# Opening of a Mamba and FP4-FFN kernel: low weight halves on GpSimd, z projections between x projections, dt pieces behind taps

## The chip, the cores and the metric

The kernel is one program on one core of a Trainium2 chip. The metric is the device time of one execution in microseconds, as the median of several executions. The core has five engines with queues of their own: TensorE (PE), VectorE (DVE), ScalarE (ACT), GpSimd (POOL) and SyncE (SP), which here only issues DMAs. They meet through semaphores.

## The reference, cut to what matters

For 8 sequences of 512 tokens with 512 features: a Mamba-2 block, residual and layer norm, then a feed-forward block with 4-bit weights, residual and layer norm.

```python
zxbcdt = u @ in_proj_w.T                      # 512 -> 64 (dt) + 128 (B) + 128 (C) + 1024 (x) + 1024 (z)
z, xBC, dt_raw = split(zxbcdt)
xBC = silu(causal_conv4(xBC) + conv_b)        # depthwise, four taps over the tokens
dt = softplus(dt_raw + dt_bias)
y = chunked_scan(x, dt, -exp(A_log), B, C)    # chunks of 64 tokens, decays exp(cumsum(dt * A))
yg = (y + x * D) * silu(z)
x1 = layernorm(u + rmsnorm(yg) * norm_weight @ out_proj_w.T)
out = layernorm(x1 + rmsnorm((silu(x1 @ gate.T) * (x1 @ up.T)) @ down.T))
```

## The kernel before, in words

Phase 1 runs the Mamba block over the 8 sequences, phase 2 the feed-forward block. While sequence b is scanned (`body`, 32 slots, four for each of 8 chunks), the input projection of sequence b+1 is made between the scan's steps. The projection of sequence 0 has nothing to hide behind: it is the opening of the program, and the change is in it alone.

The input projection has 19 output tiles of up to 128 features by 512 tokens: dt, B, C, x0 to x7, z0 to z7. Each is 12 matmuls: 4 blocks of input features, times three products of half-precision parts (`w_hi*u_hi`, `w_hi*u_lo`, `w_lo*u_hi`). The tiles take the two PSUM banks `ps_in0` and `ps_in1` in turn, by their place in a list of uses. A bank is free again when its tile has been read:

- a B, C or x tile is read by ScalarE (`take_conv`: the fourth tap, scaled, with the bias, into `pre`) and then by VectorE (`taps`: the three other taps, each an add into `pre`, the three of them in a chain). The third tap of VectorE frees the bank.
- a z tile is read by ScalarE alone (`take_z`: silu into `zg`), which frees the bank.

The weights come in as f32 and are split in the opening. `W_BLOCKS` has five blocks of columns: block 0 (dt, B, C), 1 (x0 to x3), 2 (x4 to x7), 3 (z0 to z3), 4 (z4 to z7), each of four tiles k of 128 input features. ScalarE writes `w_hi` = f16(w * scale) (`weights_hi`), VectorE writes `w_lo` = f16(w * scale - w_hi) (`weights_lo`). PE waits for a block's two halves ahead of the first tile that needs it. The f32 weights lie in buffers that are used for other things later: `xs` and the last part of `pre` (blocks 0 to 2), `zg` (blocks 3 and 4). So ScalarE must not write x5 into `pre` before all of `w_lo` of block 2 is made, nor z0 into `zg` before all of block 4's.

The time steps dt go through 25 small operations on VectorE (128x256), in pieces: `dt_first`, `dt_second` with parts 0 to 4, `dt_third`. Parts 1 to 4 are called pieces 1 to 4 below. ScalarE adds an exponential, a logarithm (`ln_dt`, after piece 3) and the factors of the scan (`exp_cs`, after the first operation of piece 4). After `dt_third` SyncE stores the parts to DRAM and loads rows back for the scan.

The opening ends in `tail`: after x7, one silu over B and C and two over x (`silu_all`) must wait for the last tap; `a0`, `a1`, `a2` are transposes and a product of chunk 0 that ScalarE evicts, `e0`, `e1`, `e2` the first exponent matrices, whose exponentials are ScalarE's. Each engine works its queue in the order of the code. GpSimd has almost nothing to do in the opening: two maxima over the partitions, a third (`reduce_u(1)`) after VectorE's `measure_u(1)`, behind the last taps.

## Time and profile before

| | us |
|---|---|
| median of 3 runs (1782.76 to 1784.73) | 1783.25 |
| the profiled execution, its own time | 1782.91 |
| its span, first to last instruction | 1781.1 |
| PE busy in the span | 1626.2 (91%) |
| DVE, POOL, ACT busy | 1304.0, 1119.5, 930.2 |
| opening, up to the first exponential of the scan's own slots | 114.0 |

How to read it: the span is one execution taken by the hardware profiler. A row of the timeline has the start in us from the span's start, the length in us, the engine, the line, the operation, the tile written and the tiles read with their shapes, the number of instructions of which the row is made, and in brackets how long the engine stood idle before and what released it. The end of a matmul is modelled; consecutive matmuls overlap, so it is their starts that count. A row of the stage view has a stretch and its length, then busy time and number of instructions of PE, PE's weight loads, DVE, ACT and POOL, then the granted clock of TensorE (1.00 is 2.4 GHz, 0.50 is 1.2 GHz), the DMA share and GB/s. Lines are those of the kernel before.

### The profile page before, as it was taken

Reading aid. Unit: us, or ns where it says so; the run is one execution under the profiler, and the core shown is the slowest. Engines: PE = TensorE matmul, PEld = TensorE weight load, DVE = VectorE, ACT = ScalarE, POOL = GpSimd, SP = SyncE. Lnnn points to the kernel's source line nnn. Section 1 sums busy time; section 2 is a strip of 40 time slices with the busy share of each in tenths; the row PEclk is TensorE's granted clock in tenths of the full one; section 3 lists DMA queues with packets and bytes.
Section 4 is the critical chain, followed back from the end, with each engine's and each line's share of the span. In section 5 each row is a group of like instructions: output and inputs, shape, how many; then the busy total and the mean of one; then the engine's idle time right before and its main releaser. Section 6 shows DMA issues by size and latency. Waiting matters only on the chain.

```text
span 1781.1 us, 36900 instructions
## 1 busy us (share of the span) xinstructions
PE 1626.2 (91%) x11168; PEld 818.8 (46%) x11168; DVE 1304.0 (73%) x2016; ACT 930.2 (52%) x1647; POOL 1119.5 (63%) x1087
## 2 busy tenths in 40 slices
PE   2699999989998998998998998888999999999998
PEld 1245545535544544544554554543344444444443
DVE  5939858858867876975985886656777777777774
ACT  2454454354445445435436436325766666666662
POOL 0038738837936845863873882885777776667773
PEclk9889999999999998998999999888999999999999
DMA  6121151141133124014114115721111101101011
GB/s 228 46 57 29 27 120 45 23 107 52 28 76 91 24 56 113 17 45 120 29 27 114 52 23 117 195 27 48 36 47 38 60 29 55 54 30 60 24 36 60
DMA packets 214697, 109.81 MB, mean 62 GB/s; under 512 B 133796, under 2 KB 185696, under 8 KB 214496
## 3 DMA queue, kind: packets, MB, share of 16 engines
q1 hardware_dynamic: 214496, 107.37, 22.5%
q8 instruction: 97, 1.59, 0.4%
q14 instruction: 104, 0.85, 0.2%
HBM read 80.57 MB, written 26.76 MB: 60 GB/s over the span
## 4 chain that ended last, share of the span: by engine, by line
PE 54%; issue 14%; DVE 12%; POOL 11%; ACT 4%; DMA 1%; SPq 1%; DVEq 0%; POOLq 0%; ACTq 0%
PE ps_in L770 12%; PE ps_in L924 8%; PE ps_yo L939 6%; PE ps_yd L939 6%; PE ps_in L792 6%; PE ps_s L924 4%; PE ps_t L924 4%; POOL xend L1665 4%; DVE pre L1270 3%; POOL y L1685 2%; PE ps_yo L850 2%; POOL y L1679 2%; DVE mix L1358 2%; PE ps_yd L840 1%; POOL sq L1702 1%
## 5 line engine op out<-in xcount | busy, mean ns | idle before, releaser
L770 PE MATMUL ps_in<-u_hi,w_hi 128*128 128x512 f16 (+1 forms) x608 | 234.3, 385 | 60.6 <-DVE u_lo L1257 32.4
L1665 POOL TENSOR_TENSOR xend<-xpad,decay 128x256 f32<-128x256 f32 x256 | 223.8, 894 | 102.9 <-PE ps_yo L863 47.1
L1075 ACT ACTIVATE decay<-ps_d 128x512 f32<-128x512 f32 x256 | 149.5, 592 | 243.6 <-PE ps_d L828 151.6
L792 PE MATMUL ps_in<-w_out,zg 128*128 128x512 f32 x512 | 230.8, 604 | 3.0 <-DVE pre L1270 2.5
L770 PE MATMUL ps_in<-u_lo,w_hi 128*128 128x512 f16 (+1 forms) x608 | 233.5, 384 | 0.0
L770 PE MATMUL ps_in<-u_hi,w_lo 128*128 128x512 f16 (+1 forms) x608 | 233.2, 383 | 0.0
L1358 DVE TENSOR_TENSOR mix<-decay,gb 128x1024 f32<-128x1024 f32 x128 | 179.3, 1401 | 49.3 <-ACT decay L1075 35.1
L1763 POOL TENSOR_TENSOR gate_sum<-gate_sum,gate_part 128x512 f32<-128x512 f32 x88 | 142.2, 1616 | 104.4 <-DVE gate_part L1586 104.0
L1270 DVE SCALAR_TENSOR_TENSOR pre<-ps_in,cws,pre 128x511 f32<-128x511 f32 (+2 forms) x240 | 179.2, 747 | 14.4 <-ACT pre L1014 8.1
L792 PEld LDWEIGHTS ps_in<-w_out,zg 128*128 128x128 f32 x512 | 95.8, 192 | 134.7 <-issue 124.2
L924 PE MATMUL ps_in<-xt_hi,gu_w 128*128 128x512 f16 x352 | 134.4, 382 | 5.5 <-DVE gate_sum L1586 2.3
L924 PE MATMUL ps_in<-xt_lo,gu_w 128*128 128x512 f16 x352 | 134.2, 381 | 0.0
L770 PEld LDWEIGHTS ps_in<-u_hi,w_hi 128*128 128x128 f16 (+1 forms) x608 | 60.8, 100 | 146.0 <-issue 46.4
L1014 ACT ACTIVATE pre<-ps_in,cb,cws 128x512 f32<-128x512 f32 x80 | 62.3, 778 | 121.7 <-PE ps_in L770 121.3
L1763 POOL TENSOR_TENSOR up_sum<-up_sum,up_part 128x512 f32<-128x512 f32 x88 | 113.0, 1284 | 14.6 <-DVE up_part L1586 14.1
L1679 POOL TENSOR_TENSOR y<-xs,dskip 128x512 f32<-128x512 f32 x64 | 80.4, 1256 | 56.5 <-issue 56.5
L850 PE MATMUL ps_yo<-bc,state 128*128 128x64 f32 x896 | 114.0, 281 | 0.9 <-DVE state L1374 0.9
L828 PE MATMUL ps_d<-rhs_d,lhs_d 94*128 94x512 bf16 x256 | 103.8, 406 | 6.9 <-DMA lhs_d<-ld_dram 6.0
L850 PEld LDWEIGHTS ps_yo<-bc,state 128*128 128x128 f32 x896 | 106.2, 194 | 6.2 <-DVE state L1374 1.2
L1671 POOL TENSOR_TENSOR state_d<-state,dec 128x1024 f32<-128x1024 f32 x48 | 104.6, 2178 | 0.0
L1771 POOL TENSOR_TENSOR h_lo<-hf,h_hi 128x512 f16<-128x512 f32 x88 | 103.1, 1172 | 0.3 <-ACT h_hi L1199 0.3
L1586 DVE SCALAR_TENSOR_TENSOR gate_part<-ps_in,gs,gate_part 128x512 f32<-128x512 f32 x88 | 66.0, 751 | 45.0 <-ACT gate_part L1185 35.5
(181 smaller groups left out, 3732.3 us busy)
## 6 DMA issues: line engine op xcount, KB each, us to landing
ebc<-e_dram SPq DMA_DIRECT2D x256, 64.0 KB, 2.7
u<-u_t SPq DMA_DIRECT2D x9, 1024.0 KB, 4.9
res<-u_tok SPq DMA_DIRECT2D x32, 256.0 KB, 3.7
x_dram<-res SPq DMA_DIRECT2D x32, 256.0 KB, 2.1
xa<-x_dram SPq DMA_DIRECT2D x8, 1024.0 KB, 5.8
xr<-x_dram SPq DMA_DIRECT2D x32, 256.0 KB, 2.6
out<-xr SPq DMA_DIRECT2D x32, 256.0 KB, 2.1
fw_words<-gu_words SPq DMA_DIRECT2D x32, 176.0 KB, 4.4
```

Of the source, the lines that this page charges most:

```text
L770: last = mm(ps_in[bk][0:m, :], w[:, k, col:col + m], u[:, k, :], start=(k == 0 and j == 0), stop=(k == KT - 1 and j == 2))
L792: last = mm(ps_in[bk][:, :], zg[:, k, tt * P:(tt + 1) * P], w_out[:, k, :], start=(k == 0), stop=(k == CT - 1))
L850: last = mm(ps_yo[:, k * CH:(k + 1) * CH], state[:, k * P:(k + 1) * P], bc[:, 1, c * CH:(c + 1) * CH], start=True, stop=True)
L924: last = mm(ps_gu[u % len(ps_gu)][:, :], gu_w[:, g, col:col + P], x[p.par][:, g, :], start=(j == 0), stop=(j == 1))
L939: last = mm(ps_n[tt % 2][:, :], h[par][:, k, tt * P:(tt + 1) * P], w[:, k, :], start=(step == 0), stop=(step == TILE_MMS - 1))
L1075: ac(decay[:, n % NG, :, :].rearrange("p a b -> p (a b)"), ps_d[n % 2][:, :], ACT.Exp).then_inc(e_done, 1)
L1270: ins = v.scalar_tensor_tensor(pre[:, m, d:L], ps_in[bk][:, 0:L - d], cws[:, m, k:k + 1], pre[:, m, d:L], ALU.mult, ALU.add)
L1358: v.tensor_tensor(mix[:, g:g + 2, :, :].rearrange("p g e t -> p (g e) t"), decay[:, g:g + 2, :, :].rearrange("p g e t -> p (g e) t"), gb[: ...
L1665: g_.tensor_tensor(xend[:, pairs, :], xpad[:, c % 2, pairs, :], decay[:, g, :, CH - 1:CH].broadcast_to([P, CT, 2 * HD]), ALU.mult).then_in ...
L1671: g_.tensor_tensor(state_d[:, :].rearrange("p (q d) -> p q d", d=HD), state[:, :].rearrange("p (q d) -> p q d", d=HD), dec[:, :, c:c + 1]. ...
L1679: g_.tensor_tensor(y[:, c % 2, :, :], xs[:, :, c * CH:(c + 1) * CH], dskip[:, :].unsqueeze(2).broadcast_to([P, CT, CH]), ALU.mult).then_in ...
L1763: g_.tensor_tensor(to[:, buf, :], to[:, buf, :], part[:, buf, :], ALU.add).then_inc(part_done, 1)
```

## The change

Three things are changed in the opening, and nothing else.

- `w_lo` of blocks 2, 3 and 4 (12 instructions of 128x512) is made by GpSimd. GpSimd gets a plain subtraction of two operands, so its f32 operand must already be scaled: ScalarE multiplies each f32 row block by `scale` in place (12 more activations, `weights_scaled`), right after the two or four `w_hi` that it makes from it. GpSimd waits for each tile's `w_hi` and for its scaled rows. ScalarE makes these blocks in smaller groups, between `take_conv` of C to x3.
- The order of the tiles is dt, B, C, x0 to x4, z0, x5, z1, x6, z2, x7, z3, z4, and then z5, z6, z7; `a0` comes after z4, and e0, a1, e1, a2, e2 after z7. Before, the order was x0 to x7, z0, a0, z1, z2, e0, a1, e1, z3, a2, e2, z4 to z7. The banks still alternate.
- VectorE makes the taps of x0 and x1 ahead of piece 1, the taps of x2 ahead of piece 2, those of x3 ahead of pieces 3 and 4, and `dt_third` after the taps of x5. ScalarE's `ln_dt` and `exp_cs` stand together after x4, ahead of z0.

```diff
@@ -73,10 +73,11 @@
 
 
 HEAD = ["a0", "z1", "z2", "e0", "a1", "e1", "z3", "a2", "e2", "z4", "z5", "z6", "z7"]
-TAIL = {"pro": ["x7", "z0"] + HEAD, "body": ["x6", "x7", "z0", "o3", "q3"] + HEAD, "last": ["o3", "q3"]}
+PRO_ORDER = ["dt", "B", "C", "x0", "x1", "x2", "x3", "x4", "z0", "x5", "z1", "x6", "z2"]
+TAIL = {"pro": ["x7", "z3", "z4", "a0", "z5", "z6", "z7", "e0", "a1", "e1", "a2", "e2"], "body": ["x6", "x7", "z0", "o3", "q3"] + HEAD, "last": ["o3", "q3"]}
 AUX_ORDER = (0, 2, 1)
 NA = len(AUX_ORDER)
-PRO_USES = [(0, "dt"), (0, "B"), (0, "C")] + [(0, f"x{i}") for i in range(CT - 1)]
+PRO_USES = [(0, name) for name in PRO_ORDER]
 BODY_USES = [(4, "dt"), (5, "B"), (7, "C"), (9, "x0"), (11, "x1"), (12, "o0"), (13, "q0"), (17, "x2"), (19, "x3"),
              (20, "o1"), (21, "q1"), (25, "x4"), (27, "x5"), (28, "o2"), (29, "q2")]
 LAST_USES = [(12, "o0"), (13, "q0"), (20, "o1"), (21, "q1"), (28, "o2"), (29, "q2")]
@@ -365,6 +366,7 @@
         w_out_done = sem("w_out_done")
         w_hi_done = sem("w_hi_done")
         w_lo_done = sem("w_lo_done")
+        w_scaled = sem("w_scaled")
         u_in = sem("u_in")
         res_in = [sem(f"res_in{tt}") for tt in range(TT)]
         rq_in = [sem("rq_in0"), sem("rq_in1")]
@@ -1125,10 +1127,16 @@
                     elif name[0] == "z":
                         take_z(st, name)
 
-            def weights_hi(block):
+            def weights_hi(block, tiles=range(KT)):
                 col, n = W_BLOCKS[block]
-                for k in range(KT):
+                for k in tiles:
                     ac(w_hi[:, k, col:col + n], w_src(k, col, n), ACT.Identity, scale=w_in_scale).then_inc(w_hi_done, 1)
+
+            def weights_scaled(block, tiles):
+                col, n = W_BLOCKS[block]
+                weights_hi(block, tiles)
+                for k in tiles:
+                    ac(w_src(k, col, n), w_src(k, col, n), ACT.Identity, scale=w_in_scale).then_inc(w_scaled, 1)
 
             act.wait_ge(small_in, N_SMALL)
 
@@ -1142,18 +1150,21 @@
             exp_dt(0)
             take_conv(pro, "B")
             take_conv(pro, "C")
-            weights_hi(2)
-            for i in range(CT - 1):
-                if i == 5:
+            weights_scaled(2, range(2))
+            for name in PRO_ORDER[3:]:
+                if name == "x5":
 
                     act.wait_ge(w_lo_done, KT * 3)
-                take_conv(pro, f"x{i}")
-                if i == 2:
+                if name[0] == "z":
+                    take_z(pro, name)
+                    continue
+                take_conv(pro, name)
+                i = int(name[1])
+                if i < 4:
+                    weights_scaled(*((2, range(2, KT)), (3, range(2)), (3, range(2, KT)), (4, range(KT)))[i])
+                if i == 4:
                     ln_dt(0)
-                if i == 4:
                     exp_cs(0)
-                if i in (3, 5):
-                    weights_hi(i // 2 + 2)
             act.wait_ge(const_in, N_CONST)
             act.wait_ge(pro_pool, 1)
             tail(pro)
@@ -1554,16 +1565,16 @@
             taps(pro, "C")
             dve.wait_ge(const_in, N_CONST)
             v.tensor_scalar(to_top[:, :], shift[:, :], 28, None, ALU.bitwise_xor)
-            dt_second(0, 1)
-            weights_lo(2)
-            for i in range(CT):
-                if i < 3:
-                    dt_second(0, 2 + i)
-                if i == 3:
-                    dt_third(0)
+            taps(pro, "x0")
+            for i in range(1, 4):
                 taps(pro, f"x{i}")
-                if i in (3, 5):
-                    weights_lo(i // 2 + 2)
+                dt_second(0, i)
+            dt_second(0, 4)
+            taps(pro, "x4")
+            taps(pro, "x5")
+            dt_third(0)
+            taps(pro, "x6")
+            taps(pro, "x7")
             measure_u(1)
             dve.wait_ge(w_out_in, 16)
             for k in range(CT):
@@ -1750,6 +1761,14 @@
             reduce_u(0)
             pool.wait_ge(pro_dve, MAXES_READY)
             g_.partition_all_reduce(maxes_all[:, :], maxes[:, :], P, RMAX).then_inc(pro_pool, 1)
+            pool.wait_ge(w_lo_done, 2 * KT)
+            for block in range(2, len(W_BLOCKS)):
+                col, n = W_BLOCKS[block]
+                for k in range(KT):
+                    pool.wait_ge(w_hi_done, KT * block + k + 1)
+                    pool.wait_ge(w_scaled, KT * (block - 2) + k + 1)
+                    g_.tensor_tensor(w_lo[:, k, col:col + n], w_src(k, col, n), w_hi[:, k, col:col + n], ALU.subtract)\
+                        .then_inc(w_lo_done, 1)
             reduce_u(1)
             body(Stage("body", 0))
             with pool.Fori(1, nb - 1) as i:
```

ScalarE before, from the taking of B and C on (`pre<-ps_in` is `take_conv`, `w_hi<-` is `weights_hi`):

```order
L1014 ACTIVATE pre<-ps_in,cb,cws 128x512 x2
L1131 ACTIVATE w_hi<-xs,scal 128x512 x3
L1131 ACTIVATE w_hi<-pre,scal 128x512
L1014 ACTIVATE pre<-ps_in,cb,cws 128x512 x3
L1006 ACT_TABLE_LOAD
L1006 ACTIVATE dtc<-dta 128x256
L1014 ACTIVATE pre<-ps_in,cb,cws 128x512
L1131 ACTIVATE w_hi<-zg,scal 128x512 x4
L1014 ACTIVATE pre<-ps_in,cb,cws 128x512
```

ScalarE now, the same place (`xs<-xs`, `pre<-pre` and `zg<-zg` are the scalings in place):

```order
L1016 ACTIVATE pre<-ps_in,cb,cws 128x512 x2
L1133 ACTIVATE w_hi<-xs,scal 128x512 x2
L1139 ACTIVATE xs<-xs,scal 128x512 x2
L1016 ACTIVATE pre<-ps_in,cb,cws 128x512
L1133 ACTIVATE w_hi<-xs,scal 128x512
L1133 ACTIVATE w_hi<-pre,scal 128x512
L1139 ACTIVATE xs<-xs,scal 128x512
L1139 ACTIVATE pre<-pre,scal 128x512
L1016 ACTIVATE pre<-ps_in,cb,cws 128x512
L1133 ACTIVATE w_hi<-zg,scal 128x512 x2
L1139 ACTIVATE zg<-zg,scal 128x512 x2
L1016 ACTIVATE pre<-ps_in,cb,cws 128x512
```

Each taking of an x tile now stands behind four activations, up to x3; eight more (block 4) stand between x3 and x4.

VectorE before, from the taps of C (a set of taps is three rows, 511, 510 and 509 elements) to the taps of x0:

```order
L1270 SCALAR_TENSOR_TENSOR pre<-ps_in,cws,pre 128x509
L1556 TENSOR_SCALAR to_top<-shift 128x1
L1290 TENSOR_TENSOR dtb<-dtb,dtd 128x256
L1291 TENSOR_TENSOR dtc<-dtb 128x256
L1292 TENSOR_SCALAR dtd<-dtc 128x256
L1293 TENSOR_TENSOR dtd<-dtd,dtc 128x256
L1543 SCALAR_TENSOR_TENSOR w_lo<-xs,scal,w_hi 128x512 x3
L1543 SCALAR_TENSOR_TENSOR w_lo<-pre,scal,w_hi 128x512
L1296 SCALAR_TENSOR_TENSOR dtd<-dtd,dtc 128x256 x5
L1270 SCALAR_TENSOR_TENSOR pre<-ps_in,cws,pre 128x511
L1270 SCALAR_TENSOR_TENSOR pre<-ps_in,cws,pre 128x510
L1270 SCALAR_TENSOR_TENSOR pre<-ps_in,cws,pre 128x509
```

VectorE now, from the last tap of x0 on:

```order
L1281 SCALAR_TENSOR_TENSOR pre<-ps_in,cws,pre 128x509
L1281 SCALAR_TENSOR_TENSOR pre<-ps_in,cws,pre 128x511
L1281 SCALAR_TENSOR_TENSOR pre<-ps_in,cws,pre 128x510
L1281 SCALAR_TENSOR_TENSOR pre<-ps_in,cws,pre 128x509
L1301 TENSOR_TENSOR dtb<-dtb,dtd 128x256
L1302 TENSOR_TENSOR dtc<-dtb 128x256
L1303 TENSOR_SCALAR dtd<-dtc 128x256
L1304 TENSOR_TENSOR dtd<-dtd,dtc 128x256
L1281 SCALAR_TENSOR_TENSOR pre<-ps_in,cws,pre 128x511
L1281 SCALAR_TENSOR_TENSOR pre<-ps_in,cws,pre 128x510
L1281 SCALAR_TENSOR_TENSOR pre<-ps_in,cws,pre 128x509
L1307 SCALAR_TENSOR_TENSOR dtd<-dtd,dtc 128x256 x5
```

The four `w_lo` and piece 2 stood ahead of the taps of x0; now those of x0, x1 and x2 come ahead of piece 2, and the `w_lo` are gone.

GpSimd before, at the program's start (`umax_all` and `maxes_all` are the maxima over the partitions; a row named ISA without a tile is an instruction that the program puts ahead of a first use of another kind):

```order
L1655 ISA umax_all<-umax 128x1
L1752 ISA maxes_all<-maxes 128x3
L1655 ISA umax_all<-umax 128x1
L1679 ISA
L1679 TENSOR_TENSOR y<-xs,dskip 128x512
L1665 TENSOR_TENSOR xend<-xpad,decay 128x256 x4
```

GpSimd now:

```order
L1666 ISA umax_all<-umax 128x1
L1763 ISA maxes_all<-maxes 128x3
L1770 ISA
L1770 TENSOR_TENSOR w_lo<-xs,w_hi 128x512 x3
L1770 TENSOR_TENSOR w_lo<-pre,w_hi 128x512
L1770 TENSOR_TENSOR w_lo<-zg,w_hi 128x512 x8
L1666 ISA
L1666 ISA umax_all<-umax 128x1
L1690 ISA
L1690 TENSOR_TENSOR y<-xs,dskip 128x512
```

The twelve subtractions stand ahead of the third maximum, with one more such ISA row ahead of them and one more ahead of that maximum.

## Rows read from the trace of the kernel before

**Rows 1.** Stage view: end of the waits inside the opening; first scan.
```profile
57.00:65.00 8.00, 7.54 (x24) 2.73 (x24) 7.58 (x15) 2.90 (x4) 0.00 (x0) 0.72 0.00 0
...
130.00:231.00 101.00, 97.77 (x842) 53.64 (x835) 85.38 (x119) 45.84 (x86) 76.77 (x81) 1.00 0.13 33
```

**Rows 2.** Timeline, TensorE: first matmul of x1, first of x2, last of x2.
```profile
47.94 0.39 PE L770 MATMUL ps_in<-u_hi,w_hi 128*128 128x512 f16 x1 [1.50 <-DVE pre L1270]
...
56.92 0.61 PE L770 MATMUL ps_in<-u_hi,w_hi 128*128 128x512 f16 x1 [6.21 <-DVE pre L1270]
...
61.57 0.38 PE L770 MATMUL ps_in<-u_hi,w_lo 128*128 128x512 f16 x1
```

**Rows 3.** Timeline, VectorE: pieces of dt, low halves and taps, x0 to x2.
```profile
47.86 0.42 DVE L1290 TENSOR_TENSOR dtb<-dtb,dtd 128x256 f32<-128x256 f32 x1
...
49.59 2.08 DVE L1543 SCALAR_TENSOR_TENSOR w_lo<-xs,scal,w_hi 128x512 f16<-128x512 f32 x3
...
52.25 2.26 DVE L1296 SCALAR_TENSOR_TENSOR dtd<-dtd,dtc 128x256 f32<-128x256 f32 x5
54.54 2.31 DVE L1270 SCALAR_TENSOR_TENSOR pre<-ps_in,cws,pre 128x511 f32<-128x511 f32 x3
56.78 0.41 DVE L1298 SCALAR_TENSOR_TENSOR dtd<-dtd,dtb 128x256 f32<-128x256 f32 x1
...
58.40 2.32 DVE L1270 SCALAR_TENSOR_TENSOR pre<-ps_in,cws,pre 128x511 f32<-128x511 f32 x3
60.63 0.68 DVE L1306 TENSOR_TENSOR_SCAN dte<-mask,dtb 128x256 f32<-128x256 bf16 x1
...
62.81 2.31 DVE L1270 SCALAR_TENSOR_TENSOR pre<-ps_in,cws,pre 128x511 f32<-128x511 f32 x3
```

**Rows 4.** Timeline, ScalarE: high halves, x1 taken, silus, first exponentials, z7, slot 0's exponential.
```profile
43.68 1.93 ACT L1131 ACTIVATE w_hi<-xs,scal 128x512 f16<-128x512 f32 x3
...
50.74 0.78 ACT L1014 ACTIVATE pre<-ps_in,cb,cws 128x512 f32<-128x512 f32 x1 [3.49 <-PE ps_in L770]
...
84.64 1.06 ACT L1025 ACTIVATE bc<-pre 128x1024 f32<-128x1024 f32 x1 [1.09 <-DVE pre L1270]
85.60 3.69 ACT L1027 ACTIVATE xs<-pre 128x2048 f32<-128x2048 f32 x2
...
98.64 0.60 ACT L1075 ACTIVATE decay<-ps_d 128x512 f32<-128x512 f32 x1
...
101.38 0.60 ACT L1075 ACTIVATE decay<-ps_d 128x512 f32<-128x512 f32 x1
...
112.01 0.69 ACT L1038 ACTIVATE zg<-ps_in,uundo 128x512 f32<-128x512 f32 x1 [1.90 <-PE ps_in L770]
...
114.01 0.60 ACT L1075 ACTIVATE decay<-ps_d 128x512 f32<-128x512 f32 x1
```

**Rows 5.** Timeline of the first scan: VectorE's rows, then GpSimd's.
```profile
132.66 2.31 DVE L1270 SCALAR_TENSOR_TENSOR pre<-ps_in,cws,pre 128x511 f32<-128x511 f32 x3
...
144.10 0.85 DVE L1290 TENSOR_TENSOR dtb<-dtb,dtd 128x256 f32<-128x256 f32 x1
144.98 1.15 DVE L1291 TENSOR_TENSOR dtc<-dtb 128x256 f32<-128x256 f32 x1
...
132.82 1.28 POOL L1685 TENSOR_TENSOR y<-y,yoff 128x512 f32<-128x512 f32 x1 [1.47 <-DVE yoff L1385]
...
143.06 1.61 POOL L1665 TENSOR_TENSOR xend<-xpad,decay 128x256 f32<-128x256 f32 x1
144.63 1.22 POOL L1679 TENSOR_TENSOR y<-xs,dskip 128x512 f32<-128x512 f32 x1
```

**Rows 6.** GpSimd: duration of `h_lo` in phase 2 (ns, min/median/max); timeline of the opening.
```profile
L1771 POOL TENSOR_TENSOR h_lo<-hf,h_hi x88: 1144/1157/1353, 1229.1 to 1749.3; 128x512 f16<-128x512 f32 x88
...
95.19 1.03 POOL L1679 TENSOR_TENSOR y<-xs,dskip 128x512 f32<-128x512 f32 x1 [7.57 <-issue]
...
115.27 2.02 POOL L1679 TENSOR_TENSOR y<-xs,dskip 128x512 f32<-128x512 f32 x1
```

## Prediction

> **What bounds the kernel now.** I read the stage view first. In the scan's stages TensorE is full: 97.77 of 101.00 us at a clock of 1.00 [rows 1]. Whatever the opening saves is therefore kept by the end if the scan only starts earlier, and nothing else in the program changes. In the opening TensorE is not the bound. The timeline of TensorE shows x1's projection at 47.94 and x2's only at 56.92, after 6.21 us of idleness that a tap of VectorE ended [rows 2]; the timeline of VectorE shows what it did meanwhile: piece 1 (47.86), four `w_lo` (49.59), piece 2 (52.25), and only at 54.54 the taps of x0, which free x2's bank [rows 3]. The opening is a chain of VectorE's work up to the last tap, then of the silus, then of the z tiles: silus from 84.64 to 89.29, z7 taken at 112.01, the exponential of slot 0 at 114.01 [rows 4]. That last row is my mark: all that follows it is the same work in both kernels. The question is when it starts now.
>
> **Prices.** Two projections stand 2.59 apart when nothing stops them (z7's taking: 1.90 idle and 0.69 of the one before) [rows 4]. From a projection's first matmul to its taking it is 2.80 (47.94 to 50.74), the taking is 0.78, a set of taps holds VectorE 2.24 (54.54 to 56.78), and the bank's next projection starts 2.38 after the taps began (54.54 to 56.92) [rows 2 to 4]. So x tiles that share one bank follow each other at 2.80 + 0.78 + 0.03 + 2.38 = 6.0 us, and a z tile (2.59) fits beside each. Pieces 1 to 4 hold VectorE 1.73, 2.29, 1.62 and 2.18 (the differences of neighbouring starts) [rows 3]. ScalarE starts its weight activations 0.61 apart (1.93 for three, overlapping by a tenth) [rows 4]. The scaling in place is not in the trace; between the 0.61 of `w_hi` and the 1.06 of the silu that writes f32 at twice the size [rows 4] I take 0.61, since shape and function are those of `w_hi`. GpSimd's `w_lo` has the form of `h_lo` (f32 and f16 in, f16 out, 128x512): 1144 to 1353 ns, median 1157 [rows 6]; the other end is the 2.02 of a product of that size that met VectorE [rows 6]. I take 1.16.
>
> **VectorE, x1 to x4.** The taps of C end at 47.86 as before; those of x0 follow at once and end at 50.1. x1 was projected at 47.94 and is taken at 50.74, so its taps start at 51.55. From there VectorE doesn't pause until x4's taps end: four sets of taps and four pieces, 4 x 2.24 + 1.73 + 2.29 + 1.62 + 2.18 = 16.8, to 68.35. The ScalarE work in between is not late: after x3 is taken (about 57) eight activations take 4.9, so x4 is taken at 62.7, and its taps come at 66 at the earliest. x4 needs block 2's `w_lo`, which GpSimd makes between 45.6 and 51.5; its projection starts at 58 or later. Block 3 is ready by 59, z0's projection comes at 62 or later.
>
> **What GpSimd costs VectorE.** In the scan, the multiplication of piece 1 at 144.10 takes 0.85 instead of 0.42; GpSimd's `xend` ends at 144.67 and VectorE 0.28 later. The next, at 144.98, takes 1.15: GpSimd's `y` ends at 145.85 and VectorE again 0.28 later [rows 3, 5]. So the pieces stand still while a GpSimd operation runs and do their streaming after it. Taps keep their 2.31 beside GpSimd's 132.82 row [rows 5]. The trace behaves as the Trainium skill states (SBUF — State Buffer, "Who interferes with whom"): a VectorE instruction with two SBUF inputs and a GpSimd one that reads SBUF exclude each other for a whole instruction. By that rule the change pays the loss worked out next; if the two engines did not exclude each other it would pay nothing, and the gain would be 3.35 larger. Walking the queues: block 3's first two `w_lo` run from 53.4 to 55.7, just when piece 1 starts (53.8); two of its operations wait, 1.5 us. Piece 2 then ends beside block 4's first `w_lo` (about 61): 0.9. Piece 3 begins beside the last: 0.95. Together 3.35, with bounds of 0 (no meeting) and 5.2 (each of about five waits a whole operation of 1.16, less what overlaps). x4's taps end at 71.7, x5's projection starts at 71.8.
>
> **TensorE's clock.** z0's projection is over by 68 or 69, so TensorE stands idle about 4 us ahead of x5. After 6.21 us of idleness it came back at half clock: x2's first matmul is 0.61 long, its last at 61.57 is back at 0.38, and the stage has 0.72 [rows 1, 2]. x2 took 4.65 from first to last start against 2.38 (2.59 less one start) at full clock, 2.3 more. For x5 I take 1.5: between 0 and 2.5, which all twelve at half clock would cost.
>
> **x5 to the mark.** x5 is as if started at 73.3; x6 at 79.3, x7 at 85.3 (two cycles of 6.0; `dt_third`, z1 and z2 lie beside them). Its last tap ends 2.80 + 0.81 + 2.24 later, at 91.15. That is 6.5 later than the 84.64 of before, but z0, z1, z2 are done and z3, z4 projected. The silus take 4.65 (84.64 to 89.29) [rows 4]: 95.8. z3 is taken (0.69), which frees the bank of z5: 96.5. Three projections, 7.8: z7's taking starts at 104.5, 0.2 after its last matmul. Then 0.69, a table load (112.01 + 0.69 to 114.01 leaves 1.3) [rows 4]: 106.5. The four exponentials, which before had their first three among the z tiles, now all stand behind z7: from 98.64 to the end of the third, 101.98, is 3.34 [rows 4], and transposes at half clock after the waits may add 0.4. The mark: 110.3 instead of 114.0, a gain of 3.7.
>
> **Costs at nothing, and their cover.** SyncE stores the dt parts about 14 us later (`dt_third` ends near 81.5), and needs about 15 us until the scan's rows are in SBUF, near 96.5; e0 asks for them near 104.5. The cover is 8 us. GpSimd's third maximum waits for `measure_u(1)`, over at about 93.5. A switch of kind costs 7.57 at 95.19 [rows 6]; two of them and the maximum end near 108.5, and `y` and the four `xend` near 112. New state is wanted some 7 us after the mark, so 5 us are left. z0's taking waits for all twelve `w_lo`, near 66, while ScalarE reaches it at 70. VectorE's `w_out` work (3.3) ends near 97.
>
> **The sum.** Without the meeting and the clock the gain would be 3.7 + 3.35 + 1.5 = 8.5; less 3.35, less 1.5: 3.7 us. Against its own time of 1782.91 that is 1779.2. The median of the runs shown is 0.34 higher, so 1779.5.
>
> **The rivals.**
> A, as forecast: gain 1.8 to 5.5. Chance 0.60.
> B, the meeting costs little, because VectorE's pieces fall between GpSimd's operations, or the clock stays up for x5: gain 5.5 to 8.5, time 1774.8 to 1777.8. For it: GpSimd is busy only 14 of the 20 us in question. Against: block 4's four run back to back into piece 3. Chance 0.20.
> C, the change moves nothing that can be told: each `w_lo` takes the 2.02 of the row at 115.27 [rows 6], so that each of four waits grows by 0.86, 3.4 in all; gain 0.3, time 1783. For it: that row shows how GpSimd itself is held. Against: VectorE's taps, most of its work there, do not hold it. Chance 0.15, with a gain between -3.6 and 1.8.
> D, slower: TensorE stays at half clock past x5. Each projection at 5.12 instead of 2.59 on the path (x5, x6, x7, z5, z6, z7) costs 2.5; one and a half more of them eat the gain, and with four more, 10.1, the time is 1789.6. It is slower by more than 0.2% from three more on. For it: every pair of tiles leaves TensorE idle 0.8 of 6.0 us, and it stands before x5 and before a0. Against: each return to work in rows 2 was back at full speed after under 5 us. Chance 0.05.
>
> **How the numbers follow.** 0.2% (3.6 us) is about what a measurement of this kernel can tell. Faster by more: half of A, the upper half of its range, and all of B: 0.5. Slower: D, 0.05. The rest, 0.45, is the lower half of A and C. The range leaves out the top of B, D, and most of C: 1776.5 to 1782.8.
>
> **What would show it.** TensorE's first x2 matmul near 50.5 instead of 56.92. VectorE unbroken from 51.5 to about 71.7, with single operations of pieces 1, 2 and 3 at 1.1 to 1.5 us instead of 0.42 beside `w_lo`. `w_lo` on GpSimd near 1.16, the last over near 66. x5 at half clock for its first part. The last tap near 91, silus after it; z7 taken near 104.5, slot 0's exponential near 110.3. The forecast is wrong if the scaling in place takes more than 1.0 (x4 would then be taken some 3 us later, at the edge of its taps), if SyncE's rows come after 104.5, or if the scan does not keep what the opening gives.

## The result

The changed kernel takes 1774.35 us (median of 5, 1773.86 to 1775.74), the kernel before 1784.73 (5 runs, 1782.76 to 1786.14). The ratio is 0.9944, interval 0.993 to 0.9959: 10 us faster, where 3.7 were forecast. The time lies below the range. The profiled execution is the one of 1774.35, its span 1772.5.

The stage view of the changed kernel, in the stretches of [rows 1]; columns are the length, then busy us (and count) of PE, PEld, DVE, ACT and POOL, TensorE's granted clock, the DMA share and GB/s:

```profile
57.00:65.00 8.00, 5.73 (x19) 2.07 (x20) 7.69 (x12) 6.50 (x10) 5.63 (x5) 0.79 0.01 2
130.00:231.00 101.00, 97.50 (x824) 52.32 (x823) 87.25 (x121) 44.65 (x83) 75.24 (x80) 1.00 0.13 33
```

GpSimd now works 5.63 of the 8 us in which it did nothing. The scan's stage looks as before. The timeline of TensorE (start, length, engine, line, operation, idle before and its releaser), first matmuls of x3, x4, z0, x5 and x6, with the last of x4 (62.08) and of x5 (75.13) and one of z5 (99.68) between them, answers to [rows 2]:

```profile
52.72 0.39 PE L772 MATMUL ps_in<-u_hi,w_hi 128*128 128x512 f16 x1 [0.63 <-DVE pre L1281]
58.31 0.38 PE L772 MATMUL ps_in<-u_hi,w_hi 128*128 128x512 f16 x1 [2.83 <-DVE pre L1281]
...
62.08 0.63 PE L772 MATMUL ps_in<-u_hi,w_lo 128*128 128x512 f16 x1
63.68 0.38 PE L772 MATMUL ps_in<-u_hi,w_hi 128*128 128x512 f16 x1 [0.96 <-DVE pre L1281]
70.46 0.61 PE L772 MATMUL ps_in<-u_hi,w_hi 128*128 128x512 f16 x1 [4.03 <-DVE pre L1281]
...
75.13 0.63 PE L772 MATMUL ps_in<-u_hi,w_lo 128*128 128x512 f16 x1
...
79.05 0.39 PE L772 MATMUL ps_in<-u_hi,w_hi 128*128 128x512 f16 x1 [0.36 <-DVE pre L1281]
...
99.68 0.63 PE L772 MATMUL ps_in<-u_hi,w_lo 128*128 128x512 f16 x1
```

x2 no longer waits, x3 waits 0.63. x4 waits 2.83, and its last seven matmuls ran at half clock (0.63 for a matmul instead of 0.38); that was off the path, because x4 was taken at 62.76 and VectorE came to its taps only at 68.10. x5 comes after 4.03 us of idleness at half clock, and all of its twelve stay there. The timeline of VectorE (answers to [rows 3]), then of GpSimd:

```profile
52.58 1.15 DVE L1301 TENSOR_TENSOR dtb<-dtb,dtd 128x256 f32<-128x256 f32 x1
53.76 1.27 DVE L1302 TENSOR_TENSOR dtc<-dtb 128x256 f32<-128x256 f32 x1
...
58.08 3.10 DVE L1307 SCALAR_TENSOR_TENSOR dtd<-dtd,dtc 128x256 f32<-128x256 f32 x5
61.21 2.32 DVE L1281 SCALAR_TENSOR_TENSOR pre<-ps_in,cws,pre 128x511 f32<-128x511 f32 x3
63.45 1.26 DVE L1309 SCALAR_TENSOR_TENSOR dtd<-dtd,dtb 128x256 f32<-128x256 f32 x1
...
68.10 2.31 DVE L1281 SCALAR_TENSOR_TENSOR pre<-ps_in,cws,pre 128x511 f32<-128x511 f32 x3
```

```profile
48.03 1.16 POOL L1770 TENSOR_TENSOR w_lo<-xs,w_hi 128x512 f16<-128x512 f32 x1 [1.16 <-ACT xs L1139]
...
52.29 2.46 POOL L1770 TENSOR_TENSOR w_lo<-zg,w_hi 128x512 f16<-128x512 f32 x2 [1.99 <-ACT zg L1139]
55.40 2.55 POOL L1770 TENSOR_TENSOR w_lo<-zg,w_hi 128x512 f16<-128x512 f32 x2 [0.66 <-ACT zg L1139]
59.74 4.68 POOL L1770 TENSOR_TENSOR w_lo<-zg,w_hi 128x512 f16<-128x512 f32 x4 [1.79 <-ACT zg L1139]
```

The pieces that meet GpSimd's `w_lo` are long, the taps beside the same rows keep 2.31. `w_lo` takes 1.16. ScalarE's timeline (answers to [rows 4]):

```profile
91.23 1.06 ACT L1027 ACTIVATE bc<-pre 128x1024 f32<-128x1024 f32 x1 [2.38 <-DVE pre L1281]
...
101.00 0.69 ACT L1040 ACTIVATE zg<-ps_in,uundo 128x512 f32<-128x512 f32 x1 [3.31 <-PE ps_in L772]
...
106.19 0.69 ACT L1040 ACTIVATE zg<-ps_in,uundo 128x512 f32<-128x512 f32 x1 [1.90 <-PE ps_in L772]
106.89 1.28 ACT L1077 ACT_TABLE_LOAD   x1
108.19 0.60 ACT L1077 ACTIVATE decay<-ps_d 128x512 f32<-128x512 f32 x1
...
110.89 1.08 ACT L1077 ACTIVATE decay<-ps_d 128x512 f32<-128x512 f32 x2
```

The mark (the fourth exponential, the second of the last row) starts at 111.39 instead of 114.01. That is 2.6 of the 8.6 us between the two spans. The rest came behind the mark. I cut the traces at rows that all kernels have, and each column is the length from one to the next: the mark, VectorE's measuring of `u` in the first scan and in the seventh (six scans between them), and the first gate matmul of phase 2. Plain copies of both kernels were run with the first experiments.

| trace | mark | to measuring of u | six scans | to gate | rest | span |
|---|---|---|---|---|---|---|
| before | 114.01 | 118.5 | 852.7 | 127.9 | 568.0 | 1781.1 |
| ctrl_before | 115.14 | 120.1 | 855.0 | 128.8 | 568.3 | 1787.4 |
| after | 111.39 | 117.5 | 846.9 | 128.1 | 568.6 | 1772.5 |
| ctrl_after | 111.39 | 119.8 | 848.9 | 130.5 | 568.9 | 1779.5 |

Six scans, in which the two programs do the same work, are 5.7 to 6.1 us shorter. In the mean of a trace all distances between ScalarE's exponentials agree to 0.1 us, but for two: the one across the loop's jump back (15.83 and 15.86 in the two traces of before, 15.19 and 15.23 in the two of after), and the one from the eighth to the ninth exponential of a scan, near the end of a stretch at half clock (5.89 and 5.86 against 5.54 and 5.71). At the jump ScalarE's table load waits. Before, then after, at the third jump, with the take of z7 ahead:

```profile
533.74 0.69 ACT L1038 ACTIVATE zg<-ps_in,uundo 128x512 f32<-128x512 f32 x1 [1.90 <-PE ps_in L770]
538.29 1.28 ACT L1075 ACT_TABLE_LOAD   x1 [3.86 <-issue]
```

```profile
528.68 0.69 ACT L1040 ACTIVATE zg<-ps_in,uundo 128x512 f32<-128x512 f32 x1 [1.90 <-PE ps_in L772]
532.39 1.28 ACT L1077 ACT_TABLE_LOAD   x1 [3.02 <-issue]
```

"issue" means that the profile shows no semaphore or engine that held it. The mean over the five jumps of a trace is 3.79 and 4.12 in the two of before, 3.09 and 3.37 in the two of after. That is 0.72 a jump, 3.6 us in all.

### The profile page after: what moved, and what is told of

Its sections match the earlier page's. It is cut to its first block, busy times and chain, and to the rows that moved or that the text cites. A ratio compares the mean times of both kernels' runs of the same rounds, so it can differ in the third digit from the quotient of the medians.

```text
span 1772.5 us, 36925 instructions
## 1 busy us (share of the span) xinstructions
PE 1625.4 (92%) x11168; PEld 818.0 (46%) x11168; DVE 1299.6 (73%) x2004; ACT 934.0 (53%) x1657; POOL 1134.6 (64%) x1099
## 3 DMA queue, kind: packets, MB, share of 16 engines
q8 instruction: 97, 1.59, 0.4%
## 4 chain that ended last, share of the span: by engine, by line
PE 53%; issue 14%; POOL 12%; DVE 12%; ACT 4%; DMA 1%; SPq 1%; POOLq 0%; DVEq 0%; ACTq 0%
PE ps_in L772 12%; PE ps_in L926 8%; PE ps_yo L941 6%; PE ps_yd L941 6%; PE ps_in L794 5%; POOL xend L1676 4%; PE ps_s L926 4%; PE ps_t L926 4%; DVE pre L1281 3%; POOL y L1696 2%; PE ps_yo L852 2%; POOL y L1690 2%; DVE mix L1369 2%; PE ps_yd L842 1%; POOL sq L1713 1%
```

## The experiments

**Parts of the change.** `pool_dt` has the change without its order of tiles; `pool_only` without the moved dt pieces too, so that the twelve `w_lo` on GpSimd and the scaling are left.

```diff
 pool_dt, against the changed kernel
-PRO_ORDER = ["dt", "B", "C", "x0", "x1", "x2", "x3", "x4", "z0", "x5", "z1", "x6", "z2"]
+PRO_ORDER = ["dt", "B", "C", "x0", "x1", "x2", "x3", "x4", "x5", "x6"]
-TAIL = {"pro": ["x7", "z3", "z4", "a0", "z5", "z6", "z7", "e0", "a1", "e1", "a2", "e2"], ...
+TAIL = {"pro": ["x7", "z0"] + HEAD, ...
 pool_only, further
-            taps(pro, "x0")
-            for i in range(1, 4):
-                taps(pro, f"x{i}")
-                dt_second(0, i)
...
+            dt_second(0, 1)
+            for i in range(CT):
+                if i < 3:
+                    dt_second(0, 2 + i)
...
```

> The kernel before, unchanged. In the first two traces the mark (slot 0's exponential) moved by 2.6 us (114.01 to 111.38), but the span by 8.6 us (1781.1 to 1772.5): about 6 us were gained in the scans of sequences 1 to 6, whose code is the same. Theory 'chance of phase': the stretches of half clock in each scan (6.8 or 10.2 us) fall differently in each execution; then repeats of this kernel scatter by several us, and the mean of more executions of before and after differ by some 3 us only. Theory 'systematic': the repeats stay within 1782.5 to 1786.5, and the trace again has the later scans at about 142.1 us each from one measuring of u to the next.

> The changed kernel, unchanged. 'Chance of phase': its median moves towards before by some us, the difference is 2 to 5 us. 'Systematic': 1773.5 to 1776 again, 9 to 11 us below before on the same chip, and the scans of sequences 1 to 6 at about 141.2 us each.

> The change without its order of tiles: x0 to x7, z0 and the tail as before, low halves on GpSimd, dt pieces behind taps. The x chain is then bound by VectorE alone, so the last tap should come some 10 us earlier than in the change (about 80), the z tiles follow the silus as before. If the interleaving of z is what gives the gain, this kernel lies between before and after: mark about 112 to 114. If taking w_lo off VectorE is what gives it, the mark is at 109 or earlier and the time is below that of the change.

> Only low halves on GpSimd with rows scaled by ScalarE; order of tiles and of VectorE's pieces as before. VectorE loses 8.2 us of w_lo of which all lay on its chain to the last tap, less up to 3 us of meeting with GpSimd: last tap 4 to 7 us earlier than 84.6, mark 4 to 7 us earlier than 114.0. If the earlier start of the scan is kept to the end one for one the time is 4 to 7 us below before.

Against 1784.46 (32 runs): ctrl_before 1784.52 (12 runs), ratio 0.9997, 0.9986 to 1.0007; ctrl_after 1776.67 (9 runs), 0.9954, 0.9939 to 0.9969; pool_dt 1780.76, 0.9981, 0.9969 to 0.9993; pool_only 1782.53, 0.9983, 0.997 to 0.9997. The marks: 115.14, 111.39, 112.82, 114.56. The gain is systematic, 7.8 us between the two copies instead of the 9 to 11 expected. pool_dt's mark is where it was expected if the z tiles between x tiles give the gain (112 to 114). pool_only missed: its silus start at 83.75, under 1 us earlier than before, where 4 to 7 were expected. VectorE lost its `w_lo`, but then waited for ScalarE: 1.86 us for the logarithm of dt, and 1.88, 1.23, 0.21 and 1.30 ahead of the taps of x4 to x7. Executions of one kernel scatter over 9 to 11 us here, so a single trace is weak evidence for 2 us; the verdicts below rest on medians and on rows. The parts bring less than the whole, and both parts already shorten the scans (851.2 and 849.3) and the wait at the jump (means 3.43 and 3.30). That spoke, without showing it, for something that goes with the program and not with the order of work.

**Delays of VectorE.** The first theory was that TensorE's clock steps decide: where the scan starts against a step, so much of it runs at half clock. Then a delay of the opening would not cost its own length. A reduction without use stands ahead of x7's taps, in both kernels (wait1 with two rows of `pre`, wait2 with four).

```diff
+            dve.wait_ge(tap3, 10)
+            v.tensor_reduce(umax[:, :], pre[:, 2:6, :], AX.XY, ALU.max, ...)
             taps(pro, "x7")
```

> The kernel before with one more reduction on VectorE (128x1024, about 1.15 us) between ScalarE's taking of x7 and its taps: the end of the opening comes 1.15 us later, nothing else changes. [...] Theory 'steps': the time does not move by 1.15 us, but by -4 to +4 with the new place. Theory 'one for one': +1.15 us, 1785.6 to 1786.3 if before is at 1784.8.

> The same with a reduction of 128x2048, about 2.25 us. 'One for one': +2.25 us. [...]

> The changed kernel with the delay of 1.15 us between the taking of x7 and its taps. 'One for one': +1.15 us against the changed kernel, that is 7 us below before. 'Steps': measuring of sequence 2 at 1.5 to 2.5 behind a step; 4 to 9 us below before.

> The changed kernel with the delay of 2.25 us: its mark then stands at about 113.6, where that of before stands at 114.0 to 115.1. 'One for one': 6 us below before. 'Steps': measuring of sequence 2 near 3 us behind a step as in before, and then the scans too are as slow as in before: 1 to 3 us below before.

Against 1784.65: before_wait1 1785.30 (1.001, 1.0 to 1.0021), before_wait2 1787.06 (1.0016, 1.0005 to 1.0028), after_wait1 1777.59 (0.9962, 0.9948 to 0.9976), after_wait2 1777.98 (0.9967, 0.9954 to 0.998). The silu started 1.63 and 2.47 later than in ctrl_before, 1.13 and 2.25 later than in after; the medians rose by 0.8 and 2.5 over ctrl_before, and by 0.9 and 1.3 over ctrl_after. Within the noise a delay costs its length or somewhat less. before_wait2 became slower and not faster, and after_wait2 stayed 6.7 us below before instead of 1 to 3, so the clock theory fell as the cause of the 6 us. Single marks do go by the clock: they moved by 1.35 and 1.64 from ctrl_before, but by -0.56 and 0.56 from after, less than the silus. (The places behind a clock step in these expectations were counted from a wrong zero; nothing here rests on them.)

**Padding, and a `w_lo` that reads nothing.** The second theory: the wait at the jump depends on where ScalarE's loop lies in its program. Tiny activations ahead of ScalarE's first exponential shift everything behind them. `no_read` asks for the price of the meeting: `w_lo` of blocks 2 to 4 is set to zero (the low halves of these blocks are left out of the computation).

```diff
 before_pad12, before_pad28, after_pad12
+            for i in range(12):
+                ac(pad[:, i:i + 1], aneg[:, :], ACT.Exp)
 no_read
-                    g_.tensor_tensor(w_lo[:, k, col:col + n], w_src(k, col, n), w_hi[:, k, col:col + n], ALU.subtract)
+                    g_.memset(w_lo[:, k, col:col + n], 0.0).then_inc(w_lo_done, 1)
```

> The kernel before with 12 tiny activations (128x1) more at the start of ScalarE's program, hidden in its 12.5 us wait for the scale. In ten traces the scans of sequences 1 to 6 differ only near the loop's jump back: ahead of the table load that follows the jump ScalarE stands 'issue' for 3.96 us on average in the four traces with ScalarE's old program, 3.24 us in the four of the change, 3.37 us in the two with low halves on GpSimd alone. Theory 'placement': this wait is the fetch of instructions after the jump, and goes with where ScalarE's loop lies, that is with how many instructions stand ahead of it. Then this kernel, with 12 more, has the wait at 3.0 to 3.5 us and is 2 to 4 us faster than before (1781 to 1783 where before is at 1784.8). Theory 'clock alone': wait and time as before, 1784.5 to 1785.3.

> The same with 28 tiny activations (about 5 us of ScalarE's wait, still hidden). 'Placement': the wait at the jump is another value again, between 2.6 and 4.4 us, and the time moves by five times the difference. 'Clock alone': as before.

> The changed kernel with 12 tiny activations more at the start of ScalarE's program. 'Placement': its wait of 3.24 us at the jump moves, to between 2.6 and 4.2 us, and the time with it, by up to 5 us either way. 'Clock alone': 1776 to 1777, as the change.

> The changed kernel in which GpSimd fills the low halves of blocks 2 to 4 with zero instead of subtracting (the low halves are left out of the result; every wait and every matmul is kept). It reads nothing from SBUF and is short. The meeting of GpSimd with VectorE's pieces goes: pieces 1, 2 and 3 take 1.73, 2.29, 1.62 us instead of 3.27, 3.13 and 2.47, x4's taps end 3.2 us earlier, the mark comes 3 to 4.5 us earlier than 111.4, near 107.5, and the time is 3 to 4.5 us below that of the change. If the meeting were off the path, the mark stays at 111.4.

Against 1784.65: before_pad12 1783.02 (0.999, 0.9976 to 1.0004), before_pad28 1783.54 (0.9988, 0.9974 to 1.0003), after_pad12 1777.16 (0.9954, 0.994 to 0.9968), no_read 1775.11 (0.9937, 0.9918 to 0.9957). Padding alone took the mean wait at the jump from 3.96 (over the four traces with before's ScalarE program) to 3.63 and 3.33, while time moved by less than it can tell; after_pad12 kept after's wait (3.26) and time. So this test left the second theory open. In no_read VectorE's pieces are as short as in [rows 3]; its timeline:

```profile
52.76 0.42 DVE L1301 TENSOR_TENSOR dtb<-dtb,dtd 128x256 f32<-128x256 f32 x1
53.21 0.43 DVE L1302 TENSOR_TENSOR dtc<-dtb 128x256 f32<-128x256 f32 x1
...
56.70 2.25 DVE L1307 SCALAR_TENSOR_TENSOR dtd<-dtd,dtc 128x256 f32<-128x256 f32 x5
```

x7 is taken at 85.00 instead of 88.07 and the mark stands at 108.32 instead of 111.39: the meeting costs 3.1 on the path up to x7. At the mark it is 3.1 against after and 1.6 against after_pad12 (mark 109.93), because z5's half-clock stretch differs among traces. The time is 1.6 lower than ctrl_after's, where 3 to 4.5 were expected, with intervals that overlap.

**The order alone, and a spread tail.** `order_dve` keeps the change's order and has all `w_lo` on VectorE again, without scaling in place. `spread` puts the first three exponentials ahead of z5's taking (in ScalarE's own order too, by lines that the diff below leaves out).

```diff
 order_dve, against the changed kernel (and without GpSimd's w_lo and ScalarE's scaling)
             taps(pro, "x0")
+            weights_lo(2)
             for i in range(1, 4):
                 taps(pro, f"x{i}")
                 dt_second(0, i)
+                if i == 2:
+                    weights_lo(3)
             dt_second(0, 4)
             taps(pro, "x4")
+            weights_lo(4)
 spread
-"pro": ["x7", "z3", "z4", "a0", "z5", "z6", "z7", "e0", "a1", "e1", "a2", "e2"]
+"pro": ["x7", "z3", "z4", "a0", "e0", "a1", "e1", "z5", "a2", "e2", "z6", "z7"]
```

> The order of the change (z tiles between x tiles, dt pieces behind taps, exponents behind z7), with the twelve low halves of blocks 2 to 4 back on VectorE, four behind x0's taps, four behind x2's second piece, four behind x4's taps, and no scaling in place. Theory 1 (the opening is a chain of VectorE's work; GpSimd only takes low halves off it and costs 3.1 back by the meeting): twelve low halves add 0.69 each to VectorE's chain, 8.3, of which the 4.0 before x5 is not hidden either; the meeting's 3.1 goes away. The exponential of slot 3 stands near 111.4 + 8.3 - 3.1 = 116.6, at or behind the 114.0 to 115.1 of the kernel before. Theory 2 (the order alone brings the gain of the opening, GpSimd's part little, as the kernel with GpSimd's part alone, 0.6 earlier, could be read): near 111 to 112. For the six scans: Theory 1s (their time goes by where the program's instructions lie, and by the length of the half-clock stretches, which goes with the order of the z tiles): the wait of ScalarE at the jump back 3.3 to 4.1, six scans 847 to 852, as either can occur; rival 2s (only what GpSimd does in the opening makes the scans shorter): six scans at 853 to 855 as before. Time by theory 1 and 1s 1781 to 1785, by theory 2 near 1777.

> The changed kernel with slot 0 to 2's exponents ahead of z5 on ScalarE and between z4, z5 and z6 on TensorE, instead of all behind z7. Theory 1 (the tail behind z7 is on the path: z7 at 106.2, the exponential of slot 3 at 111.4, 5.2 later, where the kernel before has 2.0): z7's taking stays within 1 us of 106.2, since ScalarE waits 3.3 for z5 there and the three exponentials and two table loads take some 5.8, and the exponential of slot 3 follows it by 2.0: 108.3 to 109.3, time 1774 to 1775, some 2 to 3 below the changed kernel. Rival (TensorE's z5 and z6 wait for transposes and exponents of the first chunk, which wait for the silu of the x tiles, so that z7 comes later by what the exponents save, as it would be if the two table loads and the half-clock stretch decide): z7 taken at 108.5 or later, exponential of slot 3 at 110.5 to 112, time 1776 to 1778 as the changed kernel.

Against 1785.13 (13 runs): order_dve 1763.93 (4 runs, 1762.93 to 1767.2), ratio 0.9884, 0.9864 to 0.9904; spread 1779.43 (9 runs), 0.9968, 0.9953 to 0.9982. Both expectations of order_dve were wrong: 21 us, far more than the change itself. The mark stands at 110.36, and the six scans sum to 835.9, 13 less than ctrl_after. The twelve `w_lo` did not lengthen VectorE's chain by the 8.3 us expected, because after has room there: VectorE stands idle 6.27 us ahead of x5's taps, and 2.77 in order_dve, where the last four `w_lo` (2.73) lie in that gap. The silus start at 91.89 instead of 91.23. In `spread` the rival held: z7 taken at 109.69, the mark at 111.69. At its third jump ScalarE does not wait:

```profile
523.77 0.69 ACT L1040 ACTIVATE zg<-ps_in,uundo 128x512 f32<-128x512 f32 x1 [1.90 <-PE ps_in L772]
524.48 1.28 ACT L1077 ACT_TABLE_LOAD   x1
```

The page's table of DMA queues (packets, MB, share of 16 engines) shows what is gone, in before, then in order_dve:

```profile
q8 instruction: 97, 1.59, 0.4%
q14 instruction: 104, 0.85, 0.2%
```

```profile
q14 instruction: 79, 0.65, 0.1%
```

A packet of q14 is 0.85 MB / 104 = 8 KB. There are 25 fewer. In each of the last five of the six scans q14 moves 10 packets in all kernels run up to here and 5 in order_dve: 5 x 5 = 25. In 14 us around the third jump it moved 5 in before, 4 in after and 2 in order_dve:

```profile
q14 instruction: 5, 0.04, 0.9%
```

```profile
q14 instruction: 4, 0.03, 0.9%
```

```profile
q14 instruction: 2, 0.02, 0.4%
```

The third theory: ScalarE's program is fetched in blocks of 8 KB. When the loop's instructions lie in one block fewer, they all stay, and nothing is fetched anew at each jump. In the listing of the built programs ScalarE has 306 instructions ahead of the loop in before (waits counted), 315 in after, 303 in order_dve; the traces, which record fewer, have 266, 276 and 264 ahead of the first pass, and 310 in each pass. If this count decides, padding must bring the gain to the old kernel and take it from order_dve.

**The loop fits or doesn't.** The padding stands behind ScalarE's first exponential, where it waits 12.5 us for the weights' scale; 108 in before, 99 in after, 12 in order_dve. `spread_dve_fit` joins order_dve, the spread tail and 110.

```diff
             ac(aneg[:, :], aneg[:, :], ACT.Exp).then_inc(pro_act, 1)
+            for i in range(108):
+                rows = slice(i // 64 * 32, i // 64 * 32 + 32)
+                ac(pad[rows, i % 64:i % 64 + 1], dtbias[rows, 0:1], ACT.Exp)
```

> The kernel before with 108 tiny ScalarE activations (one column each, about 0.1 us) right after its first exponential, in the 12.5 us in which ScalarE waits for the weights' scale; nothing else is changed. Theory 3 (ScalarE's program is fetched in blocks of about 8 KB, 128 instructions of 64 bytes; the loop's instructions fit into what ScalarE keeps if they lie in one block fewer, which they do in the kernel with the order alone, whose ScalarE has three instructions fewer ahead of the loop than the kernel before; 108 more are 128 less 20, so the loop's end falls below the block's border again): the instruction queue q14 moves 5 blocks per scan instead of 10, 3 around the jump back instead of 7, ScalarE's wait there falls from 4.0 to 0.5 at most, slot 0 to slot 1 takes 5.1 instead of 8.1 to 9.5, the six scans sum to 836 to 840 instead of 851 to 855, the exponential of slot 3 stays at 114 to 115.5, and the time is 1766 to 1770. Rival (the scans are shorter because of the order of work in the opening, or what GpSimd holds): 10 blocks, wait 3.6 to 4.2, six scans 851 to 855, time 1783 to 1786.

> The changed kernel with 99 of the same activations at the same place, so that its ScalarE has 108 more ahead of the loop than the kernel before. Theory 3: 5 blocks per scan, six scans 832 to 837, ScalarE's wait at the jump under 0.5, the exponential of slot 3 at 111 to 112.3, time 1760 to 1765, which is 3 to 5 below the kernel before with its 108. Rival as in the first run: time 1775 to 1779.

> The order of the change with all low halves on VectorE, and 12 of the same activations, which lifts ScalarE's count from 3 below to 9 above that of the kernel before. Theory 3: 10 blocks per scan again, ScalarE's wait at the jump 3 to 4, six scans 847 to 851, while the exponential of slot 3 stays near 110.3: time 1775 to 1778. Rival (the order of z tiles and dt pieces with VectorE's low halves makes the scans fast, by whatever way): six scans 836 and 1764 stay.

> The order of the change with all low halves on VectorE, slot 0 to 2's exponents ahead of z5 as in the run named spread, and 110 of the same activations (19 below the kernel before, modulo a block). Theory 3 with the opening's chain: 5 blocks per scan, six scans 833 to 838, exponential of slot 3 at 109 to 110.5 (the spread took 1.0 off between the first taking of dt and it), time 1762 to 1764. Rival (the spread keeps z5 to z7 behind transposes, so that nothing is gained): 1764 to 1766.

Against 1785.89 (17 runs), all on one chip:

| kernel | ScalarE ahead of loop, against before | q14 per scan | mean wait at jump | mark | six scans | time (runs) | ratio |
|---|---|---|---|---|---|---|---|
| before_fit | +108 | 5 | none | 115.31 | 837.9 | 1771.81 (6) | 0.9917, 0.9896 to 0.9939 |
| after_fit | +108 | 5 | 0.1 | 109.95 | 835.9 | 1766.89 (6) | 0.9898, 0.9878 to 0.9917 |
| order_dve_pad12 | +9 | 10 | 3.35 | 110.28 | 849.3 | 1778.97 (12) | 0.9967, 0.9955 to 0.998 |
| spread_dve_fit | +109 | 5 | none | 112.33 | 839.2 | 1769.97 (6) | 0.9913, 0.989 to 0.9935 |

Packets, waits and scans came as the third theory had them, but for the scans of spread_dve_fit (839.2, expected 838 at most). The times lie 1 to 6 us above the ranges given, and the marks of after_fit (109.95, expected 111 to 112.3) and spread_dve_fit (112.33, expected 110.5 at most) missed. In before_fit 108 activations that compute nothing make the kernel 14 us faster. Its timeline shows them, and the third jump:

```profile
13.92 10.29 ACT L1139 ACTIVATE pad<-dtbias 32x1 f16<-32x1 f32 x108
26.43 1.47 ACT L1132 ACTIVATE w_hi<-xs,scal 128x320 f16<-128x320 f32 x3 [2.22 <-DVE scal L1536]
...
534.07 0.69 ACT L1039 ACTIVATE zg<-ps_in,uundo 128x512 f32<-128x512 f32 x1 [1.90 <-PE ps_in L771]
534.88 1.28 ACT L1076 ACT_TABLE_LOAD   x1
```

In order_dve_pad12 twelve of them cost 15 us and bring the wait back:

```profile
527.84 0.69 ACT L1041 ACTIVATE zg<-ps_in,uundo 128x512 f32<-128x512 f32 x1 [1.90 <-PE ps_in L773]
531.68 1.28 ACT L1078 ACT_TABLE_LOAD   x1 [3.15 <-issue]
```

That the placement of ScalarE's loop decides is shown both ways. All kernels agree with a period of 128 instructions: 5 packets per scan at -3, +108 and +109 against before, 10 at 0, +9, +11, +12, +21 and +28. These places alone would also fit a period of 256. What tells the two apart, beside the 8 KB of a packet, are the places of the five packets that are gone in the fitting kernels. Counted in ScalarE's recorded instructions of a pass they start at 1, 10, 59, 182 and 308 in before, at 1, 10, 46, 173 and 301 in after, and at 1, 10, 33, 161 and 287 in before_pad28: the last three lie 123 to 128 apart and move with the placement. The five packets that remain in every kernel are then another engine's; they stand still against VectorE's instructions in before and before_fit (1, 7, 100, 228, 354), which suggests VectorE's loop.

The Trainium skill (Advanced Engine Details and Errata, "ISA Cache") states 32 KB, but 128 KB on TensorE, in only two lines of 16 KB with 256 instructions each, and that the block sizes can be set per engine. That makes 64 bytes an instruction, which agrees with 8 KB and 128. Its line size is not what q14 shows here; q8 does move 16 KB a packet (1.59 MB / 97).

The best version is order_dve, at 0.9884; it is 10 to 13 us below the two medians of the changed kernel. Its 4 runs and after_fit's 6 are on different chips, so the 3.0 between them are not a direct comparison. The spread tail is no gain: its z7 comes at 109.7 and 110.3, 3.5 to 4.1 later than in after.

## Why the prediction was wrong

**The failed step** is "Whatever the opening saves is therefore kept by the end if the scan only starts earlier, and nothing else in the program changes", and behind it "all that follows it is the same work in both kernels". The work is the same, but it does not take the same time. Of the 8.6 us between the spans 2.6 lie ahead of the mark, 1.0 between it and the first measuring of `u`, 5.7 in the six scans, and -0.7 behind them. Of the 5.7, 3.6 are the shorter wait of ScalarE at five jumps back. What the runs show in place of the step: the opening's number of ScalarE instructions decides where the loop lies in blocks of 128, and that is worth up to 15 us. It was luck that the change's nine more helped, since nobody had placed them. Before lies in the worst place that was seen (3.96), after in a slightly better one (3.24 over the four traces with its ScalarE program), order_dve in the good one. Why the wait differs among kernels that all fetch 10 packets is argued: before's loop ends at most three instructions past a border, so the block behind it is fetched just ahead of the jump and the jump's own block waits for it. The packets speak for that. In all 20 jumps of the four traces with before's ScalarE program one starts 0.7 to 1.2 us ahead of the branch, in none of the 20 with after's. The first packet behind the branch then starts 2.52 us after it in the mean, instead of 1.90, and the table load 2.06 and 1.95 us after that packet. No run separates this from other effects of the placement.

**The other 2 us of the scans** stay open. In the traces TensorE's half-clock stretches at the scans' heads are longer before (10.2 against 6.8 us) in 5 scans of the two traces against 1 of after's two. They may be the answer, since the second of the two distances that differ lies there, but no run isolates them. With ScalarE's fetches gone, before_fit and after_fit still differ by 2.0, and single traces scatter by as much.

**The opening** came out near the forecast, as a sum of terms of which some were off both ways. With ScalarE's fetches gone, on one chip, after_fit is 4.9 below before_fit in time and 5.4 at the mark; ctrl_before and ctrl_after differ by 3.8 at the mark, the first two traces by 2.6. Forecast: 3.7. The scatter goes with the half-clock stretches of the opening, so part of the agreement in any one pair is luck.

- The meeting: pieces 1, 2 and 3 hold VectorE 3.27, 3.13 and 2.47 from start to start, 1.54, 0.84 and 0.85 more than before. That is 3.2, against 3.35 forecast (1.5, 0.9, 0.95), and no_read found 3.1 on the path up to x7. The rule of the Trainium skill that the prediction names (SBUF — State Buffer, "Who interferes with whom") agrees: taps beside the same `w_lo` keep 2.31.
- x4's taps end at 70.4 (forecast 71.7) and x5 starts at 70.46 (71.8): the whole opening runs 1.2 earlier in this trace, from its first taking of dt at 36.51 instead of 37.71. Its dt tile was back at full clock after seven of its twelve matmuls, before's only behind all. That is not the change's doing: after_fit took dt at 37.52.
- x5 at half clock was the term of 1.5, and is mis-sized: all twelve matmuls ran at half clock, 2.5. z5 ran at half clock for the larger part as well, which the forecast did not have; ScalarE waited 3.31 for it instead of 1.90. Together 2.5 + 1.4 against 1.5.
- The silus start at 91.23 (forecast 91.15), z7 is taken at 106.19 (104.5), the mark is 5.2 later (5.8). z7 is late by z5's half-clock stretch (after_fit, whose z5 ran at full clock, took z7 at 104.75); the 1.0 by which x5's exceeded its term was made up by the earlier start.
- `w_lo` takes 1.16, the last ends at 64.4 (forecast 66). Scaling in place starts every 0.61. Rival C did not occur, nor D.
- GpSimd's maximum and `y` were forecast ready near 112; `y` starts at 108.52 after 8.50 us of "issue". The slack held.
- GpSimd's part of the change, which the sum charged with 3.35, gives nothing that can be told: order_dve_pad12, the same order with `w_lo` on VectorE, has its mark 1.1 ahead of ctrl_after and a time 2.3 above it, with intervals that overlap. Among kernels that fit, order_dve has its mark 0.4 behind after_fit and a time 3.0 below it. The order of tiles and dt pieces brings the opening's gain.

## What to carry to other kernels

Before a small gain ahead of a loop is put down to the work that was moved, compare the instruction queues' packets per iteration and the "issue" wait behind the jump: a few instructions more or less on an engine ahead of a loop can be worth more than the change. Where a loop of some 300 instructions waits there, try shifting it by padding in idle time, or by dropping instructions. And price an idle TensorE by up to the whole projection that follows at half clock, and look for each place where it stands idle: x4, x5 and z5 all had such a stretch here, and two of the three counted.

## What the runs showed of the hardware that was not expected

- ScalarE waits 2.6 to 4.7 us for nothing but issue behind the jump back of a loop of some 310 executed instructions, and not at all when the loop fits. The six scans are 11 to 17 us shorter when it fits (after to after_fit 11.0 and 13.0, order_dve_pad12 to order_dve 13.4, before to before_fit 14.8 and 17.1), 2.2 to 3.4 for each of the five jumps.
- Padding of 32x1 or 128x1 activations costs 0.095 us apiece (10.29 for 108).
- GpSimd's change from the maximum over partitions to elementwise work shows as "issue": 7.57 us in before and 8.50 in after.

```profile
99.64 0.38 POOL L1666 PARTITION_ALL_REDUCE umax_all<-umax  x1 [35.21 <-issue]
108.52 1.03 POOL L1690 TENSOR_TENSOR y<-xs,dskip 128x512 f32<-128x512 f32 x1 [8.50 <-issue]
```
